# Non-local attention block: the first row of negated maxima sent from ScalarE's DMA queue, the second row's remainder taken one finish earlier

## The reference

```python
theta = einsum(x, W_theta)                 # 1024 queries x 32
phi   = maxpool2x2(einsum(x, W_phi))       # 256 keys x 32
g     = maxpool2x2(einsum(x, W_g))         # 256 keys x 128
beta  = softmax(theta @ phi.T, axis=-1)    # 1024 x 256
out   = gamma * ((beta @ g) @ W_o) + x
```

## Time and profile before

| | |
|---|---|
| median of 3 runs | 258.08 us (257.52 to 259.65) |
| profiled execution, its own time | 257.59 us |
| its span, first to last instruction | 255.8 us |
| busy in the span: PE, DVE, POOL, ACT | 235.7, 205.9, 168.5, 148.2 us |
| granted TensorE clock, mean | 0.998 of full speed |
| HBM traffic | 198 GB/s over the span |

### The profile page before, as it was taken

One profiled execution on the slowest core, in us unless ns is written; L12 is line 12 of the kernel. 1 busy time (PEld: TensorE's weight loads), 2 busy tenths in 40 slices (PEclk: granted clock), 3 DMA queues, 4 the chain that ended last, 5 costly groups with the idle time before them and its releaser, 6 DMA issues.

```text
span 255.8 us, 4332 instructions
## 1 busy us (share of the span) xinstructions
PE 235.7 (92%) x1464; PEld 209.1 (82%) x1464; DVE 205.9 (81%) x473; ACT 148.2 (58%) x275; POOL 168.5 (66%) x119
## 2 busy tenths in 40 slices
PE   7787989999999999999999999999979999999685
PEld 4575888988888898888889798888968888898574
DVE  4597978979889797988979797887959889798645
ACT  2762947658473756748375674837548473725160
POOL 1694696866668685766869586676946678634370
PEclk9999999999999999999999999999999999999999
DMA  7790019377492937649183765919276392807824
GB/s 239 273 363 7 0 33 343 124 196 297 94 341 78 331 151 224 271 121 373 40 302 155 254 244 130 366 52 340 104 230 263 112 322 95 299 3 279 297 85 166
DMA packets 15078, 51.14 MB, mean 200 GB/s; under 512 B 1872, under 2 KB 2512, under 8 KB 15056
## 3 DMA queue, kind: packets, MB, share of 16 engines
q1 hardware_dynamic: 14624, 50.21, 56.1%
q10 hardware_dynamic: 432, 0.66, 0.7%
HBM read 33.95 MB, written 16.78 MB: 198 GB/s over the span
## 4 chain that ended last, share of the span: by engine, by line
DVE 45%; PE 25%; DMA 13%; issue 8%; POOL 4%; ACT 3%; DVEq 0%; ACTq 0%
DVE neg_parts L577 14%; DMA theta<-neg_lo 11%; PE proj L197 10%; PE out L301 9%; DVE out L552 8%; DVE theta L558 7%; DVE g_max L570 7%; DVE y_sb L603 5%; PE shift L274 4%; DMA x_t<-in_xt 2%; POOL e_lo L506 2%; POOL x_lo L501 2%; DVE neg_lo L584 2%; DVE r_sum L594 1%; PE shift L301 1%
## 5 line engine op out<-in xcount | busy, mean ns | idle before, releaser
L506 POOL TENSOR_TENSOR e_lo<-e_sb,e_hi 128x512 fp32r<-128x512 f32 x64 | 81.8, 1292 | 60.8 <-ACT e_sb L434 60.8
L501 POOL TENSOR_TENSOR x_lo<-x_t,x_hi 128x1024 fp32r<-128x1024 f32 x31 | 74.2, 2398 | 13.5 <-ACT x_hi L393 13.5
L301 PE MATMUL out<-G_hi,e_lo 128*128 128x258 f32 x188 | 53.2, 283 | 0.5 <-POOL e_lo L506 0.5
L301 PE MATMUL out<-G_hi,e_hi 128*128 128x258 f32 x188 | 53.3, 284 | 0.0
L301 PE MATMUL out<-G_lo,e_hi 128*128 128x258 f32 x188 | 53.3, 283 | 0.0
L431 ACT ACTIVATE e_hi<-shift 128x512 fp32r<-128x512 f32 x64 | 38.5, 602 | 23.6 <-PE shift L274 23.6
L197 PE MATMUL proj<-x_hi,w_hi 128*128 128x512 f32 x122 | 48.5, 397 | 3.1 <-DVE theta L558 2.3
L603 DVE SCALAR_TENSOR_TENSOR y_sb<-out,r_sum,x_n 128x256 f32<-128x256 f32 x94 | 45.5, 484 | 6.4
L197 PE MATMUL proj<-x_hi,w_lo 128*128 128x512 f32 x122 | 48.2, 395 | 0.0
L197 PE MATMUL proj<-x_lo,w_hi 128*128 128x512 f32 x122 | 48.1, 395 | 0.0
L577 DVE TENSOR_REDUCE neg_parts<-score 128x2 f32<-128x512 f32 x64 | 43.7, 686 | 1.3 <-PE score L231 0.4
(11 more groups left out here) (81 smaller groups left out, 389.4 us busy)
## 6 DMA issues: line engine op xcount, KB each, us to landing
x_n<-in_xn SPq DMA_DIRECT2D x32, 512.0 KB, 7.2
x_t<-in_xt SPq DMA_DIRECT2D x31, 512.0 KB, 5.3
out<-y_sb SPq DMA_DIRECT2D x31, 512.0 KB, 6.3
x_t<-in_xt ACTq DMA_DIRECT2D x2, 256.0 KB, 4.8
w_sb<-in_w_proj SPq DMA_DIRECT2D x1, 256.0 KB, 3.8
theta<-neg_hi SPq DMA_DIRECT2D x16, 4.0 KB
theta<-neg_lo SPq DMA_DIRECT2D x16, 4.0 KB
out<-y_sb SPq DMA_DIRECT2D x1, 256.0 KB, 2.4
```

Of the source, the lines that this page charges most:

```text
L301: last = nc.tensor.matmul(out_bank(i, t)[:, 0:GW], e[:, i % 2, KC * h + k, cells], G[:, i % 3, k, :], start=(n == 0), stop=(n == 3 * KC - 1))
L501: nc.gpsimd.tensor_tensor(x_lo[:, i % 2, h], x_t[:, i % 2, h], x_hi[:, i % 2, h].bitcast(f32), ALU.subtract).then_inc(x_lo_ready, 1)
L506: nc.gpsimd.tensor_tensor(e_lo[:, i % 2, n, :], e_sb[:, n, :], e_hi[:, i % 2, n, :].bitcast(f32), ALU.subtract).then_inc(e_lo_ready, 1)
```

## The change

`neg_hi` is sent by ScalarE's queue directly behind `neg_high`, which first waits for its own result; SyncE keeps only `neg_lo`. VectorE's `neg_low(b)` moves from behind finish 2 to behind finish 1 in steps 2 to 15. The number of DMAs, their sizes and the semaphore that they raise stay.

```diff
+        def max_row(i, r):
+            return theta[THETA + r:THETA + r + 1, i % 3, :].bitcast(f32).rearrange("r (t n) -> r t n", t=TILES)
...
             def max_into_stack(i):
-                def row(r):
-                    return theta[THETA + r:THETA + r + 1, i % 3, :].bitcast(f32).rearrange("r (t n) -> r t n", t=TILES)
-
-                sp.wait_ge(neg_hi_ready, i + 1)
-                sp.dma_start(row(0), neg_hi[:, :].bitcast(f32)).then_inc(neg_in[i % 3], 16)
                 sp.wait_ge(neg_lo_ready, i + 1)
-                sp.dma_start(row(1), neg_lo[:, :].bitcast(f32)).then_inc(neg_in[i % 3], 16)
+                sp.dma_start(max_row(i, 1), neg_lo[:, :].bitcast(f32)).then_inc(neg_in[i % 3], 16)
...
                 nc.scalar.copy(neg_hi[:, :], neg_bank[0:TILES, 0:P]).then_inc(neg_hi_ready, 1)
+                act.wait_ge(neg_hi_ready, i + 1)
+                act.dma_start(max_row(i, 0), neg_hi[:, :].bitcast(f32)).then_inc(neg_in[i % 3], 16)
...
-                finishes(d, (0, 1, 2))
+                finishes(d, (0, 1))
                 neg_low(b)
                 if a < LAST:
-                    finishes(d, (3, 4, 5))
+                    finishes(d, (2, 3, 4, 5))
                     G_low(a)
                     finishes(d, (6, 7))
                 else:
-                    finishes(d, (3, 4))
+                    finishes(d, (2, 3, 4))
                     maxima(a, 0)
```

## The result

The changed kernel took 249.28 us in the median of 4 runs (248.00 to 249.95), the kernel before 258.27 beside it (257.52 to 259.65). The ratio is 0.964 with a 95% interval of 0.9581 to 0.9699. In a second set (experiment e0) it was 250.0 against 256.94, ratio 0.9709 (0.9662 to 0.9756). The forecast was 250.9 with a range from 249.4: the sign and the place were right, the gain in the first set was larger than said, 9.0 instead of 7.2 us. The profiled execution took 248.00 us, with a span of 246.2.

The account below looks back on a forecast made before the run. A loop of VectorE, row DMA and TensorE closing at `shifted(b, 0)`, with TensorE nearly full. 12 x 0.59 + 0.1 = 7.2 us off 257.59 gives 250.4; the median, 0.5 above, is forecast at 250.9, range 249.4 to 253.4.

Parts of the forecast that it names:

- What bounds: Regular step of 14.80 us: VectorE 9.4, DMA 1.8, TensorE 3.6 in a loop closing at `shifted`; TensorE nearly full.
- Part 1: VectorE's `neg_low` moved behind finish 1: `neg_lo` starts 0.59 us earlier per step, at no cost.
- The room of 0.61: TensorE before `shifted`: the next matmul could start at 126.51 instead of 127.12, 0.61 us per step.
- Part 2: Row 0 (`neg_hi`) through ScalarE's queue: SyncE is free to issue `neg_lo` about 0.60 us earlier; ScalarE's 0.64 issue is hidden.
- The lock that the Trainium skill describes: Two issuing sequencers share a descriptor generator; overlapping issues would lose 0.03 to 0.05 us per step, some 0.5 in all.
- step 15's gain is given back there, all but 0.1: At the last image's landing, traffic beginning with step 15's half store stays in place, so step 15 adds only 0.1 us.
- the stretch before the last image longer by 0.5: Sign expected in the profile after: this stretch grows by 0.5 us and does not get shorter.
- The instruction packet: One landing at 184.56 took 2.94 instead of 1.76 us; 1.2 us once, kept in the sum, open both ways.
- Row 0 landing last: Rival: ScalarE's queue needs over 2.38 us for row 0; at 2.6 the gain is 0.37 per step, 253.6 us; chance 0.08.
- the pair in flight together: Rival: rows 0.6 us apart on two queues; one holds up the other by the whole 0.6, giving 258; chance 0.07.
- the slower case: Rival: row 0 lands later than row 1 did before; at 3.3 us, 13 steps lose 0.33 each, 262.4; chance 0.04.
- two prolonged steps in a row from packets: Rival: two more steps meet an instruction packet, 2 x 1.2 us, giving 253.3; chance 0.08.

Follow-up runs that it names:

- e0: The changed kernel run again without edits: 250.0 us (247.44 to 250.71), ratio to the kernel before 0.9709.
- e1: Against the kernel before, only neg_low moved behind finish 1, both rows on SyncE: 250.44 us, ratio 0.9705.
- e6: Against the changed kernel, neg_low moved one finish earlier, behind finish 0: 248.45 us, ratio to the kernel before 0.9664.
- e2: Against the changed kernel, neg_low put back behind finish 2, so only row 0's move to ScalarE's queue remains: 257.25 us, ratio to the kernel before 1.0006.
- e10: The reorder alone once more (kernel before with neg_low behind finish 1, both rows on SyncE): 250.67 us, one run.
- e4: Against the changed kernel, row 0 of the last image put back on SyncE: 249.79 us (248.03 to 250.68).
- e7: The kernel before run again without edits: 260.29 us, one run.
- e5: Against the changed kernel, row 1 also sent through ScalarE's queue, behind row 0: 248.12 us, ratio to the kernel before 0.967.
- e11: The queue change alone once more (row 0 on ScalarE, neg_low behind finish 2): 258.30 us, one run.

## Why the prediction was wrong, step by step

- **What bounds: right.** The loop of VectorE, DMA and TensorE closed at `shifted(b, 0)`, and with it shortened TensorE's order took its place at once (80% of the chain).
- **Part 1: right in place and size.** 0.59 was forecast per step, 0.575 to 0.59 came. e1 has nearly all of it. The room of 0.61 was nearly the right bound: e6 moved `neg_lo` further and got 0.1 more, 14.80 to 14.12 in all, because the weight load of `shifted` then starts ahead of it. The prediction's room left that out.
- **Part 2: right.** Worth 0.04 per step beside part 1 (e1), nothing alone (e2). ScalarE's issue of 0.66 was hidden, and row 0 did not land last. The lock that the Trainium skill describes (Perfetto Trace Analysis, DMA Instruction — HWDGE (DVE, Sync)) was priced in the prediction at 0.03 to 0.05 per step, an estimate. No cost of it shows: in the changed kernel ScalarE issues until 122.22 and SyncE from 122.19 for 0.65. In e6 SyncE's issue starts 0.31 behind ScalarE's, well inside it, and takes 0.65 too, as it does in e2, where it starts 1.2 behind.
- **The failed step of the sum: "step 15's gain is given back there, all but 0.1".** I took the last landing for the end of a backlog that begins with the half store of step 15. It isn't. With the landing in the long band, the stretch was 10.95, 10.76 and 11.04 with the reorder (e1, e10, e4), against 10.91 and 11.12 without (the first trace of before and e7). If the traffic had been fixed in time it would have been about 11.4. The loads x_n(15) are issued behind finish 7 of image 13, so they move with `shifted` (3.30 us behind it in the trace of before, 3.44 in the changed kernel's), and the landing moves with them. The sign "the stretch before the last image longer by 0.5" did not come: it was 1.2 shorter. This term was 0.5 us; the sum should have been 13 x 0.59 = 7.7, and the forecast 250.4.
- **A term that I did not have: the last landing has two bands.** I read 3.95 us from one execution and treated it as a quantity. The first trace after the change had 2.60, and its last stretch is 1.2 of its gain. The prediction blamed the loads ahead in the queue; e5, e0 and e11 point to the DMA engines instead.
- **The instruction packet: kept in, rightly on the average, not in the first trace.** Fourteen profiles were taken. A regular landing was prolonged by 1.1 to 1.9 us in ten of them, once each, and always in step 4 or in step 12. In each of the ten, seven of row 1's eight 512 B packets start on time and the eighth starts within 0.06 us of the end of an instruction packet. The other instruction packets that pass while row 1 is moved leave all eight on time, and `shifted` starts as in any step. The trace of before has two such, in steps 4 and 8, beginning at 66.92 and 126.13, as close behind the issue (0.8 us) as the one that counted; the changed kernel's first trace has two, beginning 0.67 and 0.72 behind it. So the packets come near the row in steps 4, 8 and 12, and what varies is whether one is in the way of one of the eight. That they meet on one DMA engine is read from these times; the trace does not name the engine, and no run took the packet away. The prediction had the row stand behind that one packet for 1.2 us, which is right in cause and loose in size: in its trace the eighth packet started 0.4 us late, and the other 0.8 came behind that start. What they are is open. So is why a packet is in the way in one execution and not in the next.
- **Together.** The profiled executions differ by 9.6: 7.5 for 13 steps, 1.2 for the packet, 1.2 for the last stretch, less 0.3 at the start, where two executions of one kernel differ as much (38.37 in the first trace of before, 38.80 in e7). Several runs of the changed kernel are near 247.5 and others near 250. e0's profile shows one way to such a distance, a packet (1.6) and a long last landing (1.1). e4's shows another: no step prolonged, a long landing and the lower clock behind it, 249.67. For the runs without a profile it is not shown which it was. Which mixture a set of four or six runs catches moves the median: 9.0 faster in one set, 6.9 in the other, on either side of the corrected 7.7. So beyond the 0.5 of the failed step, how far the first set fell below the forecast is luck; the second set's 250.0 is inside the range. My range allowed one such term downwards, not two.
- **The rivals.** Row 0 landing last, the pair in flight together and the slower case did not occur: in the regular steps `shifted` started 1.81 or 1.82 us behind row 1's issue, 1.80 before the change. No profile had two prolonged steps in a row from packets.

Open: why one or two DMA engines are more than 1 us further behind at the last row in seven of eleven profiles, and why five of five profiles with row 0 on SyncE are among the seven.

## What to carry to other kernels

A small transfer at the end of a chain is worth as much as the wait of the engine behind it, and no more: read the distance from that engine's last useful instruction to its late one, and take the smaller of that and of what the producer can be moved by. Moving the producer up in its engine's list gave it all here; moving an issue to another queue gave nothing until the issues touched. Before counting on a landing time under load, take it from several executions, and look first at what is in flight ahead of it: one load of 512 KB moved behind the row was worth more than a queue of its own. And where a small transfer is late, count its packets: here one or two of eight were late, in either queue.

## What the runs showed of the hardware

- A 4 KB transfer from 8 partitions into one took 1.75 to 1.78 us from issue to landing on either queue when the DMA engines were idle, and 2.6 to 4.2 us with two 512 KB loads ahead. On a queue without the loads it still took 2.64 (e5).
- It was moved in 8 packets of 512 B, and it landed behind the last of them. Where one of the eight started at the end of an instruction packet of 0.02 MB, the landing took 2.8 to 3.7 us (ten cases); where such a packet passed and all eight were on time, it was not prolonged.
- Issues on ScalarE and SyncE that overlapped by 0.3 us took no longer than alone (0.65 on SyncE in e6 and in e2).
- Behind four waits of TensorE its granted clock fell to 0.50 for about 3 us: 1.82 us (e7, step 12) and 2.15, 2.22 and 2.40 (e1, e4 and e7, last image). Behind waits of 1.95, 1.98, 2.19 and 2.19 at the same place (e0, e10, the first trace of before, e11) it stayed at 1.00. So the length of the wait alone does not decide.
- Two matmuls of 512 columns took 0.73 us where their weight load started with them, and 0.63 where it started 0.12 us ahead (e6).
